# One core's vision transformer block: another order of the steps, and the row maxima transposed in float16

## The chip, the cores and the metric

The kernel runs on one core of one Trainium2 chip. The metric is the device time of one execution, in microseconds; the median of several executions counts.

## The reference, cut to what matters

64 images are computed one by one, and nothing is shared between them but the weights.

```python
h = layernorm(patches(x)) @ W + b          # 768 -> 192, then a second layernorm, class token first: 197 rows
h = h + attention1(layernorm(h))           # 12 heads of 64; q, k scaled by their norm over the heads
h = h + attention2(layernorm(h))           # 12 heads of 16; qkv = x@Wqkv + top-2 gated low-rank term
# attention1: q = q * rsqrt(norm(q, over heads) + eps), k the same
#   softmax(q k^T / scale[h]) v, then @ w_out.T + b_out
# attention2: probs = softmax(x@Wg + bg); two largest gates; h = x@A + ba; delta = 2*((h*gate)@Bm + gate@bb)
#   softmax(q k^T * 16**-0.5) v, then @ Wproj.T + bproj
```

## The kernel before, in words

The 197 rows of an image stand as two tiles of 98 and 99 rows. Five engines work side by side: TensorE (PE) multiplies into the 8 banks of PSUM, VectorE (DVE) and ScalarE (ACT) read the products, GpSimd (POOL) does a few sums and the inverse roots of the layer norms, and SyncE loads and stores images.

All engines walk one list of steps, `ORDER`. The list is one half of a pass, and it is worked off once for each image (64 halves, after some steps ahead and before some behind). Each name is a step: the sign says for which image it is done in this half (none: the half's own image, `+` the next, `-` the one before, `=` two before), the number after the dot is the part, and the number after `@` is the first PSUM bank that the step's product takes. **An engine does its share of the steps strictly in the order of the list.** Semaphores hold it back where an input is not there, or where the bank is not yet read out. The wait for a bank is placed by a helper that looks up the step that used the bank before, and who reads that step's product.

The steps, with what each engine does (the line numbers are those of the profile):

| step | PE | then |
|---|---|---|
| X | | ACT squares the image (L786), POOL sums the squares (L501 to L503) |
| EMB | embedding, float32 (L590, L600) | DVE L1039 to L1046, POOL inverse root (L519, L522) |
| LA, LB, LC | | DVE, two more norms (L1056, L1064, L1069, L1008, L1011, L1017), each with POOL's inverse root between |
| T1, T2 | transposes of the normalised rows (L563) | ACT high half (L796, for T2 L794 too), then DVE low half (L1083) |
| QK.0 to .2 | q and k, two banks each (L612) | ACT squares and copies (L802, L806, L809, L811) |
| S, PS | PS sums over heads (L617) | S: DVE L1094 to L1096; PS: ACT four functions (L822 to L826) |
| N.0 to .3 | | DVE L1102, L1107, L1114; ACT casts (L831) |
| V, V2 | values (L622; L732, L735) | ACT (L835; L890) |
| SM, SM2 | scores for the maxima, 64 rows (L631), 32 rows (L639) | DVE maximum (L1119; twice L1132), the last with the sign change (L1126, L1140) |
| NT, NT2 | transposes of the negated maxima (L552) | ACT (L841, L844) |
| ST, ST2 | scores to exponentiate (L656, L660; L674) | ACT exponentials into four buffers (L850, for ST2 twice) |
| PV, PV2 | sums and values (L686; L744), 32 columns of the array a head | ACT and DVE (L860, L861; L1221, L865, L866), then M and M2: DVE (L1149; L1228) |
| OP, OP2 | output products (L695; L751) | DVE adds (L1158, with variance; L1233) |
| LD, G, GB, T3 | gates (L705), transposes (L552, L713) | DVE L1017, L1167 to L1172, L1177 to L1194, L1200 and L1201 |
| QK2.0, .1 | q and k of the second attention (L722, L725) | ACT L881, L886, L887, then DVE L1207, L1211 |

Three shapes of matmul use the array in parts: SM and ST put two products side by side on 64 rows each, SM2 and ST2 four on 32 rows each, PV and PV2 four on 32 columns each. All others take all rows and columns.

POOL adds the biases in LC and LD (L508, L513), on its own queue and in the order of the list.

Of the kernel before, what the change touches and what calls it, by code (L numbers as in the profile page):

```python
# [27 lines left out]
NT = NP + 1  # L28
PD, KC = 768, 6
TR, TO = 99, 98  # L30
H, DH = 12, 64
# [17 lines left out]


ORDER = """
+X T1@4 =QK2.0@1 =QK2.1@0 QK.0@2 =SM2.0@4 QK.1@0 QK.2@2 =SM2.1@4 -ST.3@0 -ST.4@4 -ST.5@2 -PV.1@6 S
-M.1 =SM2.2@0 -PV.2@4 PS@1 =NT2@7 -M.2 N.0 N.1 N.2 +EMB@2 -OP@3 N.3 =ST2.0@4 V.0@0 SM.0@2 =ST2.1@4
-LD =V2@0 SM.1@4 SM.2@2 -T2@6 =PV2.0@7 SM.3@4 =M2.0 =ST2.2@0 =PV2.1@6 SM.4@4 SM.5@0 -G@7 =PV2.2@2
NT@4 V.1@0 ST.0@4 =M2.1 ST.1@6 +LA =M2.2 -GB +LB ST.2@2 =OP2@5 -T3@4 +LC PV.0@6 M.0
"""


# [17 lines left out]
POS = {p: n for n, p in enumerate(SCHED)}  # L76
# [77 lines left out]
def vit_tower(nc, x_t, w_emb, ln1, ln1_bias, tok_const, tok_bias, w_qk, w_v, w_out, w_gl, w_qkv2, w_lora_b,  # L154
              w_bias2, w_proj, scale, row_const, mats, head_rows, out):
    F32, F16 = mybir.dt.float32, mybir.dt.float16
    ALU, ACT, AX = mybir.AluOpType, mybir.ActivationFunctionType, mybir.AxisListType
    ctx = ExitStack()
    with ctx:
        def sb(name, shape, dt=F32):  # L160
            return ctx.enter_context(nc.sbuf_tensor(name, shape, dt))

        def two(name, shape, dt=F32):
            return [sb(f"{name}{s}", shape, dt) for s in range(2)]
# [25 lines left out]
        ident, pair_sum = mats_sb[:, 0:128], mats_sb[:, 128:256]  # L190
        masks = mats_sb[:, 256:260]
        low_row = sb("low_row", [128, 2])

        bias_rows, low_gates = slice(64, 64 + GROWS), slice(96, 96 + NE + 1)
        one_col = emb_w[:, 0, D:D + 1]
# [37 lines left out]
        vx = [vx_both[0:TR, s] for s in range(2)]  # L233
        ones_col = sb("ones_col", [TR, DH // 2])
        mx = two("mx", [TR, 2, H])
        neg = two("neg", [TR, 2, 128])
        mx2, neg2 = two("mx2", [TR, 2, H]), two("neg2", [TR, 2, 128])
        ebufs = sb("ebufs", [128, EBUFS, 2, 2, NT])
        ebuf = [ebufs[0:TR, i] for i in range(EBUFS)]
        rinv = two("rinv", [128, NT])  # L240
# [101 lines left out]
        def wait(eng, now, sig, p, earlier=None, by=1):  # L342


            n = now.count(steps[sig[0]], p, earlier)
            if n is not None:
                eng.wait_ge(sig[1], n * by)

        def reader(p, bank=None):

            if p[0] in QUAD and bank is not None and bank < BANK[p] + 2:
                return rd_lo[p[0]], p
            return rd_sig[p[0]], ({"PV": "M", "PV2": "M2"}.get(p[0], p[0]), *p[1:])

        def wait_free(eng, now, order, freed):


            q, earlier = now.previous(order, now.at)
            wait(eng, now, *freed(q), earlier)

        def passes(eng, body):
            body(Pass("start", -1))
# [15 lines left out]
        for j in range(4):  # L378
            loads.append((sel2_raw[32 * j:32 * j + 32], head_rows[64:96, 0:G2]))
            for u in range(2):  # L380
                g, r = divmod(head2(u, j), 4)
# [15 lines left out]
        for part in range(3):  # L397
            r = slice(64 + GPITCH * part, 64 + GPITCH * part + NE + 1)
# [17 lines left out]
        def key_rows(t):  # L416
            return TO if t == 0 else TR
# [110 lines left out]
        def _(pe):  # L528
# [4 lines left out]
            for c in range(KC):  # L533
                nc.tensor.matmul(psum[0:TR, spare, D:2 * D], ln1b_raw[:, c, :], emb_raw[:, c, :],
                                 start=(c == 0), stop=(c == KC - 1))
# [12 lines left out]
            def transposes(p, src, width):  # L548

                for t in range(2):  # L550
                    n = key_rows(t)
                    last_mm = nc.tensor.transpose(ps(p, slice(0, width), slice(TO * t, TO * t + n)),  # L552
                                                  src(t, n), ident[0:n, 0:n])
                return last_mm
# [12 lines left out]
            def body(now):  # L567
                for p in now.steps():
# [12 lines left out]
                            pe.wait_ge(setup_dve, 5)  # L581

                    freed = [(b, *now.previous(users[b], p)) for b in banks(p)]
                    for sig, q, earlier in dict.fromkeys((*reader(q, b), earlier) for b, q, earlier in freed):
                        wait(pe, now, sig, q, earlier)
                    if kind == "EMB":
                        pe.wait_ge(x_loaded[s], (now.image(p) + 1) * 16)
                        for t in range(2):
                            for c in range(KC):
                                nc.tensor.matmul(ps(p, slice(0, TR), slice(194 * t, 194 * t + D + 1)),  # L590
                                                 xb[s][:, c, tile_cols(t)], emb_w[:, c, :],
                                                 start=(c == 0), stop=(c == KC - 1))
                        if s == 0 and now.image(p) == 0:
                            for c in range(KC):
                                mm = nc.tensor.matmul(psum[0:TR, spare, 0:D], ones, emb_w[:, c, 0:D],
                                                      start=(c == 0), stop=(c == KC - 1))
                            mm.then_inc(setup_pe, 1)
                        wait(pe, now, xss_ready, ("X", s, 0))
                        for t in range(2):
                            mm = nc.tensor.matmul(ps(p, slice(0, TR), slice(194 * t + 193, 194 * t + 194)),  # L600
                                                  xss[s][:, tile_cols(t)], one_col,
                                                  start=True, stop=True)
                    elif kind == "T1":
                        wait(pe, now, hn_ready, ("LC", s, 0))
                        mm = hidden_transposed(now, p, hn_both[s], hn_doubled, ("LC", s, 0))
                    elif kind == "QK":
                        wait(pe, now, rd_sig["T1"], ("T1", s, 0))
                        for m in range(4):
                            f = 128 * (4 * i + m)
                            at = NT * (m % 2)  # L610
                            for n, (w, v, c) in enumerate(PACKED):
                                mm = nc.tensor.matmul(ps(p, slice(0, 128), slice(at, at + NT), m // 2),  # L612
                                                      qk_w[:, w, f:f + 128], hn_s[s][:, v, c, 0:NT],
                                                      start=(n == 0), stop=(n == 4))
                    elif kind == "PS":
                        wait(pe, now, ss_ready, ("S", s, 0))
                        mm = nc.tensor.matmul(ps(p, slice(0, 128), slice(0, 2 * NT)), pair_sum,  # L617
                                              ss[s][:].rearrange("p a t -> p (a t)"), start=True, stop=True)
                    elif kind == "V":
                        for b in range(2):  # L620
                            for n, (w, v, c) in enumerate(PACKED):
                                mm = nc.tensor.matmul(ps(p, slice(0, TR), slice(0, INNER // 2), b),  # L622
                                                      hn_s[s][:, v, c, tile_cols(i)],
                                                      v_w[:, w, INNER // 2 * b:INNER // 2 * (b + 1)],
                                                      start=(n == 0), stop=(n == 4))
                    elif kind == "SM":
                        wait(pe, now, high_N, ("N", s, 3))
                        for t in range(2):
                            for e in range(2):
                                r = slice(64 * e, 64 * e + 64)  # L630
                                mm = nc.tensor.matmul(ps(p, slice(0, TR), slice(NT * t, NT * t + NT), e),  # L631
                                                      qh[r, i, tile_cols(t)], kh[r, i, 0:NT],
                                                      start=True, stop=True)
                    elif kind == "SM2":
                        wait(pe, now, high_QK2, ("QK2", s, 1))
                        for t in range(2):
                            for j in range(4):
                                r = slice(32 * j, 32 * j + 32)
                                mm = nc.tensor.matmul(ps(p, slice(0, TR), slice(NT * t, NT * t + NT), j),  # L639
                                                      qh2[s][r, i // 2, tile_cols(t)], kh2[s][r, i, 0:NT],  # L640
                                                      start=True, stop=True)
                    elif kind in ("NT", "NT2"):
                        wait(pe, now, mx_ready if kind == "NT" else mx2_ready, p)
                        table = (neg if kind == "NT" else neg2)[s]
                        mm = transposes(p, lambda t, n: table[0:n, t], 128)
                    elif kind == "ST":
                        wait(pe, now, qkn_ready, ("N", s, 3))
                        wait(pe, now, rd_sig["NT"], ("NT", s, 0))
                        for t in range(2):
# [3 lines left out]
                            for n, (left, right) in enumerate(terms):  # L653
                                for e in range(2):
                                    r = slice(64 * e, 64 * e + 64)
                                    nc.tensor.matmul(ps(p, slice(0, TR), slice(NT * t, NT * t + NT), e),  # L656
                                                     left[r], right[r], start=(n == 0), stop=False)
                            for e in range(2):
                                r = slice(64 * e, 64 * e + 64)
                                mm = nc.tensor.matmul(ps(p, slice(0, TR), slice(NT * t, NT * t + NT), e),  # L660
                                                      head_sel[r, 2 * i + e, :], neg_t[s][r, 0:NT],
                                                      start=False, stop=True)
                    elif kind == "ST2":
                        wait(pe, now, rd_sig["QK2"], ("QK2", s, 1))
                        wait(pe, now, rd_sig["NT2"], ("NT2", s, 0))
                        for t in range(2):
# [4 lines left out]
                            for n, (left, right) in enumerate(terms):  # L671
                                for j in range(4):
                                    r = slice(32 * j, 32 * j + 32)
                                    mm = nc.tensor.matmul(ps(p, slice(0, TR), slice(NT * t, NT * t + NT), j),  # L674
                                                          left[r], right[r], start=(n == 0), stop=(n == 3))
                    elif kind == "PV":
                        wait(pe, now, rd_sig["ST"], ("ST", s, 2 * i + 1))
                        wait(pe, now, rd_sig["V"], ("V", s, 1))
                        for c in (2, 0, 1):
                            for t in range(2):  # L680
                                n = key_rows(t)
                                for j in range(4):
# [3 lines left out]
                                    mm = nc.tensor.matmul(  # L686
                                        ps(p, slice(32 * j, 32 * j + 32), slice(NT * (c % 2), NT * (c % 2) + NT), c // 2),
                                        left, eb[0:n, j % 2, t, :], start=(t == 0), stop=(t == 1))
                            if c == 2:
                                mm.then_inc(sums_made[1], 1)  # L690
                    elif kind == "OP":
                        wait(pe, now, rd_sig["PV"], ("M", s, 2))
                        for t in range(2):
                            for m in range(H // 2):
                                mm = nc.tensor.matmul(ps(p, slice(0, TR), slice(D * t, D * t + D)),  # L695
                                                      o_t[s][:, m, tile_cols(t)], out_w[:, m, :],
                                                      start=(m == 0), stop=(m == H // 2 - 1))
                    elif kind == "T2":
                        wait(pe, now, hn2_ready, ("LD", s, 0))
                        mm = hidden_transposed(now, p, hn_both[s], hn2_doubled, ("LD", s, 0))  # L700
                    elif kind == "G":
                        wait(pe, now, rd_sig["T2"], ("T2", s, 0))
                        for t in range(2):
                            for c in range(2):
                                mm = nc.tensor.matmul(ps(p, slice(0, TR), slice(136 * t, 136 * t + 136)),  # L705
                                                      hn2_t[s][:, c, tile_cols(t)], gl_w[:, c, :],
                                                      start=(c == 0), stop=(c == 1))
                    elif kind == "T3":
                        wait(pe, now, hw_ready, ("GB", s, 0))
                        transposes(p, lambda t, n: hw[s][0:n, t], 128)  # L710
                        for t in range(2):
                            n = key_rows(t)
# [24 lines left out]
                    elif kind == "PV2":  # L737
                        wait(pe, now, rd_sig["ST2"], ("ST2", s, i))
                        wait(pe, now, rd_sig["V2"], ("V2", s, 0))
                        for t in range(2):  # L740
                            n = key_rows(t)
# [155 lines left out]
        def _(dve):  # L897
# [58 lines left out]
            def weights_of_scores():  # L956
                split_packed(qk_w, qk_raw)

                nc.vector.tensor_scalar(scale_sb[:], scale_sb[:], WS, None, ALU.mult).then_inc(setup_w, 1)
                splits[0] += 1  # L960
                dve.wait_ge(setup_w, splits[0])
                nc.vector.reciprocal(inv_scale[:], scale_sb[:])
                nc.vector.tensor_copy(head_sel[:], sel_raw.broadcast_to([128, H, TR])
                                      ).then_inc(setup_dve, 1)

# [339 lines left out]
```

## Time and profile before

| | us |
|---|---|
| median of 3 executions | 3112.13 (3110.72 to 3112.16) |
| the profiled execution, its own time | 3109.35 |
| its span, first to last instruction | 3107.6 |
| PE busy in the span | 2962.8 (95%) |
| DVE busy | 2329.0 (75%) |
| ACT busy | 1963.4 (63%) |
| POOL busy | 594.1 (19%) |

Busy means that at least one instruction of the engine is under way. A matmul's record reaches from its start to its modelled end, and the next starts long before that, so what PE needs for a step is read from one step's start to the next one's.

### The profile page before, as it was taken

How to read it: one execution, taken by the hardware profiler on the slowest of the kernel's cores; microseconds unless marked ns; L12 is line 12 of the kernel's file. 1: busy time of each engine (PE TensorE's matmuls, PEld its weight loads, DVE VectorE, ACT ScalarE, POOL GpSimd, SP SyncE). 2: the span in 40 equal slices, each digit the busy share in tenths (PEclk: the TensorE clock that was granted, in tenths of full speed). 3: DMA queues.
4: the chain of work that ended last, by engine and by line, in shares of the span. 5: the costliest groups of instructions: out<-in, count | busy, mean ns of one | idle time of the engine just before them, and what ended most of it. 6: DMA issues, size and time to landing. Idle time of an engine off the chain costs nothing.

```text
span 3107.6 us, 98361 instructions
## 1 busy us (share of the span) xinstructions
PE 2962.8 (95%) x41624; PEld 2428.5 (78%) x41624; DVE 2329.0 (75%) x5441; ACT 1963.4 (63%) x3777; POOL 594.1 (19%) x859
## 2 busy tenths in 40 slices
PE   5899999999999999999999999999999999999996
PEld 4788878877877877877877877888788778778775
DVE  5777777777777777777777777777777777777773
ACT  2566666666666666666666666666666666666663
POOL 3112112111111121121121121121121111111210
PEclk7999999999999999999999999999999999999998
DMA  4000000000000000000000000000000000000000
GB/s 116 9 22 22 12 22 16 17 22 12 21 22 12 21 22 12 22 22 12 22 22 12 22 22 12 22 22 12 22 15 18 22 12 21 22 12 22 14 4 7
DMA packets 28389, 61.28 MB, mean 20 GB/s; under 512 B 4210, under 2 KB 18389, under 8 KB 27958
## 3 DMA queue, kind: packets, MB, share of 16 engines
q1 hardware_dynamic: 27958, 54.98, 6.1%
q8 instruction: 337, 5.52, 0.7%
q14 instruction: 94, 0.77, 0.1%
HBM read 45.29 MB, written 9.68 MB: 18 GB/s over the span
## 4 chain that ended last, share of the span: by engine, by line
PE 59%; DVE 35%; ACT 3%; issue 3%; POOL 0%; DMA 0%; SPq 0%; DVEq 0%; ACTq 0%
PE psum L686 9%; DVE mx L1119 8%; PE psum L695 8%; PE psum L590 8%; PE psum L612 7%; PE psum L674 4%; PE psum L722 4%; PE psum L622 4%; DVE st L1008 3%; PE psum L656 3%; DVE mx L1132 2%; PE psum L725 2%; DVE qk L1211 2%; PE psum L732 2%; PE psum L617 2%
## 5 line engine op out<-in xcount | busy, mean ns | idle before, releaser
L850 ACT ACTIVATE ebufs<-psum 99x788 f32<-99x788 f32 x768 | 592.0, 823 | 57.9 <-PE psum L674 45.2
L519 POOL TENSOR_TENSOR veps<-mv,eps_ln 99x2 f32<-99x2 f32 x256 | 116.7, 456 | 2266.5 <-DVE mv L1041 1344.9
L1132 DVE TENSOR_REDUCE mx<-psum 99x4 f32<-99x788 f32 x384 | 357.5, 974 | 137.5 <-PE psum L639 137.2
L1119 DVE TENSOR_REDUCE mx<-psum 99x4 f32<-99x788 f32 x384 | 362.9, 974 | 52.1 <-PE psum L631 52.1
L612 PE MATMUL psum<-hn_s,qk_w 128*128 128x197 f16 x3840 | 354.1, 249 | 14.9 <-DVE hn_s L1083 7.4
L612 PEld LDWEIGHTS psum<-hn_s,qk_w 128*128 128x128 f16 x3840 | 322.2, 97 | 35.6 <-DVE qk L1211 19.0
L686 PE MATMUL psum<-ebufs,vx 98*32 98x197 f32 (+1 forms) x6144 | 293.7, 330 | 0.0
L590 PE MATMUL psum<-emb_w,xb 128*99 128x193 f32 x1536 | 264.0, 327 | 0.0
L695 PE MATMUL psum<-out_w,qk 128*99 128x192 f32 x1536 | 263.8, 328 | 0.1
L590 PEld LDWEIGHTS psum<-emb_w,xb 128*99 128x99 f32 x1536 | 249.1, 166 | 1.4 <-issue 0.9
L686 PEld LDWEIGHTS psum<-ebufs,vx 98*32 98x32 f32 (+1 forms) x6144 | 201.4, 110 | 57.2
L695 PEld LDWEIGHTS psum<-out_w,qk 128*99 128x99 f32 x1536 | 245.1, 166 | 0.3 <-issue 0.3
L622 PE MATMUL psum<-v_w,hn_s 128*99 128x384 f16 x1280 | 233.9, 330 | 0.0
L656 PE MATMUL psum<-qh,kh 64*99 64x197 f16 x1536 | 207.9, 255 | 17.9 <-DVE mx L1132 17.0
L1102 DVE TENSOR_TENSOR qk<-qk,ss 128x1182 f32<-128x1182 f32 x64 | 89.1, 1392 | 167.3 <-ACT ss L826 167.3
L802 ACT ACTIVATE qk_sq<-psum 128x788 f32<-128x788 f32 x192 | 158.8, 827 | 70.3 <-PE psum L612 70.3
L656 PE MATMUL psum<-ql,kh 64*99 64x197 f16 x1536 | 201.6, 245 | 0.0
L660 PE MATMUL psum<-neg_t,head_sel 64*99 64x197 f16 x1536 | 201.4, 245 | 0.0
L656 PE MATMUL psum<-qh,kl 64*99 64x197 f16 x1536 | 201.3, 245 | 0.0
L622 PEld LDWEIGHTS psum<-v_w,hn_s 128*99 128x99 f16 x1280 | 154.8, 127 | 47.2
L831 ACT CAST kh<-qk 128x1182 f16<-128x1182 f32 x64 | 75.5, 1180 | 176.4 <-DVE qk L1107 176.4
L1149 DVE TENSOR_TENSOR qk<-psum,rinv 128x394 f32<-128x394 f32 x192 | 108.9, 567 | 101.8 <-ACT rinv L861 62.1
(172 smaller groups left out, 6442.7 us busy)
## 6 DMA issues: line engine op xcount, KB each, us to landing
xb<-x_t SPq DMA_DIRECT2D x64, 591.0 KB, 3.8
out<-h SPq DMA_DIRECT2D x128, 73.5 KB
out<-h SPq DMA_DIRECT2D x64, 0.8 KB
vx<-w_qk SPq DMA_DIRECT2D x2, 384.0 KB, 7.8
qk_sq<-w_emb SPq DMA_DIRECT2D x1, 576.0 KB
vx<-w_qk SPq DMA_DIRECT2D x1, 576.0 KB, 5.6
out_w<-w_out SPq DMA_DIRECT2D x8, 72.0 KB
late<-w_lora_b SPq DMA_DIRECT2D x1, 480.0 KB
```

Source lines behind the costliest of these rows:

```text
L590: nc.tensor.matmul(ps(p, slice(0, TR), slice(194 * t, 194 * t + D + 1)), xb[s][:, c, tile_cols(t)], emb_w[:, c, :], start=(c == 0), stop=( ...
L612: mm = nc.tensor.matmul(ps(p, slice(0, 128), slice(at, at + NT), m // 2), qk_w[:, w, f:f + 128], hn_s[s][:, v, c, 0:NT], start=(n == 0), s ...
L622: mm = nc.tensor.matmul(ps(p, slice(0, TR), slice(0, INNER // 2), b), hn_s[s][:, v, c, tile_cols(i)], v_w[:, w, INNER // 2 * b:INNER // 2 ...
L656: nc.tensor.matmul(ps(p, slice(0, TR), slice(NT * t, NT * t + NT), e), left[r], right[r], start=(n == 0), stop=False)
L660: mm = nc.tensor.matmul(ps(p, slice(0, TR), slice(NT * t, NT * t + NT), e), head_sel[r, 2 * i + e, :], neg_t[s][r, 0:NT], start=False, sto ...
L674: mm = nc.tensor.matmul(ps(p, slice(0, TR), slice(NT * t, NT * t + NT), j), left[r], right[r], start=(n == 0), stop=(n == 3))
L686: mm = nc.tensor.matmul(ps(p, slice(32 * j, 32 * j + 32), slice(NT * (c % 2), NT * (c % 2) + NT), c // 2), left, eb[0:n, j % 2, t, :], sta ...
L695: mm = nc.tensor.matmul(ps(p, slice(0, TR), slice(D * t, D * t + D)), o_t[s][:, m, tile_cols(t)], out_w[:, m, :], start=(m == 0), stop=(m ...
L802: nc.scalar.activation(qk_sq[:, 4 * i:4 * i + 4, :].rearrange("p (b m) t -> p b (m t)", b=2), src, ACT.Square, scale=1 / WS)
L850: nc.scalar.activation(ebuf[n].rearrange("p e a t -> p e (a t)"), psum[0:TR, b + 2 * half:b + 2 * half + 2, 0:2 * NT], ACT.Exp).then_inc(r ...
L1119: nc.vector.tensor_reduce(mx[s][:, :, 2 * i:2 * i + 2].rearrange("p a e -> p e a"), psum[0:TR, b:b + 2, 0:2 * NT].rearrange("p e (a t) -> ...
L1132: nc.vector.tensor_reduce(mx2[s][:, :, at:at + 2].rearrange("p a e -> p e a"), psum[0:TR, b + 2 * half:b + 2 * half + 2, 0:2 * NT].rearran ...
```

## The change

The list of steps is another one: other neighbours, other banks, and T1, NT, SM.4, SM.5, ST.0 to ST.2, PV.0, M.0 and T3 are done in another half relative to their image. The tables of the negated maxima (`neg`, `neg2`) become float16, and their transposes NT and NT2 are float16 matmuls with a float16 identity, which DVE makes once. A helper `release` is put around the two look-ups of who frees a bank or buffer; it corrects the count of a semaphore where the freeing step stands later in the list than the waiting one.

```diff
 ORDER = """
-+X T1@4 =QK2.0@1 =QK2.1@0 QK.0@2 =SM2.0@4 QK.1@0 QK.2@2 =SM2.1@4 -ST.3@0 -ST.4@4 -ST.5@2 -PV.1@6 S
--M.1 =SM2.2@0 -PV.2@4 PS@1 =NT2@7 -M.2 N.0 N.1 N.2 +EMB@2 -OP@3 N.3 =ST2.0@4 V.0@0 SM.0@2 =ST2.1@4
--LD =V2@0 SM.1@4 SM.2@2 -T2@6 =PV2.0@7 SM.3@4 =M2.0 =ST2.2@0 =PV2.1@6 SM.4@4 SM.5@0 -G@7 =PV2.2@2
-NT@4 V.1@0 ST.0@4 =M2.1 ST.1@6 +LA =M2.2 -GB +LB ST.2@2 =OP2@5 -T3@4 +LC PV.0@6 M.0
+=T3@5 -SM.4@0 -SM.5@6 QK.0@2 QK.1@4 QK.2@6 =QK2.0@2 -NT@1 S =QK2.1@4 -ST.0@6 -ST.1@2 -ST.2@0 -ST.3@6
+-PV.0@2 +X -M.0 =SM2.0@4 -ST.4@0 PS@3 -ST.5@4 =SM2.1@0 -PV.1@6 -PV.2@2 -M.1 N.0 -M.2 =SM2.2@4 N.1
+N.2 +EMB@1 N.3 =NT2@2 -OP@6 =ST2.0@0 =ST2.1@4 +LA -LD =V2@1 SM.0@4 SM.1@2 +LB V.0@6 -T2@4 =ST2.2@0
+=PV2.0@6 =PV2.1@7 +LC -G@5 =M2.0 =PV2.2@4 SM.2@0 V.1@2 =M2.1 =M2.2 -GB SM.3@0 +T1@7 =OP2@4
 """
...
+        ident_h = sb("ident_h", [TR, TR], F16)
...
-        neg = two("neg", [TR, 2, 128])
-        mx2, neg2 = two("mx2", [TR, 2, H]), two("neg2", [TR, 2, 128])
+        neg = two("neg", [TR, 2, 128], F16)
+        mx2, neg2 = two("mx2", [TR, 2, H]), two("neg2", [TR, 2, 128], F16)
...
+        def release(q, freed, earlier):
+
+            sig, r = freed
+            assert earlier or POS[r] >= POS[q]
+            return sig, r, earlier and POS[r] >= POS[q]
+
         def wait_free(eng, now, order, freed):
             q, earlier = now.previous(order, now.at)
-            wait(eng, now, *freed(q), earlier)
+            wait(eng, now, *release(q, freed(q), earlier))
...
-                    for sig, q, earlier in dict.fromkeys((*reader(q, b), earlier) for b, q, earlier in freed):
+                    for sig, q, earlier in dict.fromkeys(release(q, reader(q, b), earlier) for b, q, earlier in freed):
                         wait(pe, now, sig, q, earlier)
...
                         table = (neg if kind == "NT" else neg2)[s]
-                        mm = transposes(p, lambda t, n: table[0:n, t], 128)
+                        for t in range(2):
+                            n = key_rows(t)
+                            mm = nc.tensor.matmul(ps(p, slice(0, 128), slice(TO * t, TO * t + n)),
+                                                  table[0:n, t], ident_h[0:n, 0:n], start=True, stop=True)
...
                 nc.vector.reciprocal(inv_scale[:], scale_sb[:])
+                nc.vector.tensor_copy(ident_h[:], ident[0:TR, 0:TR])
```

## Rows read from the trace of the kernel before

**Rows 1.** The page: busy us, share of the span and instructions of each engine.

```profile
PE 2962.8 (95%) x41624; PEld 2428.5 (78%) x41624; DVE 2329.0 (75%) x5441; ACT 1963.4 (63%) x3777; POOL 594.1 (19%) x859
```

**Rows 2.** Timeline of PE, same step one image apart (start; us from first start to last end).

```profile
1500.18 4.10 PE L590 MATMUL psum<-emb_w,xb 128*99 128x193 f32 x24
...
1547.19 4.10 PE L590 MATMUL psum<-emb_w,xb 128*99 128x193 f32 x24
```

**Rows 3.** Timeline of PE, shapes that meet: scores, values, transposes.

```profile
1511.04 0.37 PE L631 MATMUL psum<-kh,qh 64*99 64x197 f16 x4
1511.34 0.46 PE L674 MATMUL psum<-qk 32*99 32x197 f16 x12
...
1513.61 0.55 PE L631 MATMUL psum<-kh,qh 64*99 64x197 f16 x8
1514.09 0.56 PE L563 MATMUL psum<-mats_sb,hn 98*128 98x98 f32 x4
...
1541.63 0.88 PE L686 MATMUL psum<-ebufs,ones_col 98*32 98x197 f32 x16
1542.33 1.53 PE L686 MATMUL psum<-ebufs,vx 98*32 98x197 f32 x32
1543.79 0.38 PE L639 MATMUL psum<-qk 32*99 32x197 f16 x8
...
1547.01 0.34 PE L552 MATMUL psum<-mats_sb,neg 98*128 98x98 f32 x2
```

**Rows 4.** Timeline of PE, where a step stood waiting.

```profile
1515.39 0.37 PE L631 MATMUL psum<-kh,qh 64*99 64x197 f16 x4
1516.11 0.46 PE L674 MATMUL psum<-qk 32*99 32x197 f16 x12 [0.34 <-issue]
...
1538.98 0.29 PE L656 MATMUL psum<-qh,kh 64*99 64x197 f16 x2
...
1540.14 0.29 PE L656 MATMUL psum<-qh,kh 64*99 64x197 f16 x2 [0.28 <-DVE mx L1132]
```

**Rows 5.** Timeline of DVE, after the output product and in the second part of a half.

```profile
1555.97 0.55 DVE L1158 TENSOR_TENSOR h<-psum,h 99x384 f32<-99x384 f32 x1
...
1557.38 1.36 DVE L1114 TENSOR_TENSOR kl<-qk,kh 128x1182 f16<-128x1182 f32 x1
...
1561.04 1.86 DVE L1119 TENSOR_REDUCE mx<-psum 99x4 f32<-99x788 f32 x2 [0.78 <-PE psum L631]
1562.82 0.56 DVE L1083 TENSOR_TENSOR hn_s<-psum,hn_s 128x394 f16<-128x394 f32 x1
...
1568.49 0.73 DVE L1056 SCALAR_TENSOR_TENSOR lnt<-lnt,rstd,emb_b 99x192 f32<-99x192 f32 x2
...
1570.08 0.33 DVE L1228 TENSOR_TENSOR late<-psum,late 128x197 f32<-128x197 f32 x1
...
1572.22 0.74 DVE L1064 SCALAR_TENSOR_TENSOR h<-lnt,mv,tokc 99x192 f32<-99x192 f32 x2
...
1574.59 0.53 DVE L1233 TENSOR_TENSOR h<-psum,h 99x384 f32<-99x384 f32 x1
```

**Rows 6.** Timeline of POOL: inverse roots and a bias.

```profile
1557.54 1.25 POOL L519 TENSOR_TENSOR veps<-mv,eps_ln 99x2 f32<-99x2 f32 x1 [1.08 <-DVE mv L1011]
...
1560.34 1.00 POOL L513 TENSOR_TENSOR h<-h,rowc 99x384 f32<-99x384 f32 x1 [0.79 <-DVE hn L1017]
...
1574.76 0.19 POOL L519 TENSOR_TENSOR veps<-mv,eps_ln 99x2 f32<-99x2 f32 x1 [3.54 <-DVE mv L1011]
1575.03 0.69 POOL L522 TENSOR_TENSOR rstd<-veps,half_neg 99x2 f32<-99x2 f32 x1
```

**Rows 7.** Timeline of ACT: the four functions of PS, the next step, exponentials.

```profile
1547.21 0.59 ACT L822 ACTIVATE ss<-psum,tiny 128x394 f32<-128x394 f32 x1 [1.44 <-PE psum L617]
...
1549.49 0.31 ACT L844 CAST neg_t<-psum 128x197 f16<-128x197 f32 x1
...
1556.41 1.55 ACT L850 ACTIVATE ebufs<-psum 99x788 f32<-99x788 f32 x2 [0.24 <-PE psum L674]
```

## The prediction, made before the changed kernel was run

> **What bounds the kernel now.** I read the page first, then the timelines of each engine over two neighbouring images, then the table of waits for the places where PE stands. PE is busy 95% of the span, DVE 75%, ACT 63% [rows 1]. The timeline of PE repeats: EMB starts at 1500.18 and at 1547.19, so one image takes 47.01 us [rows 2]. 64 of these are 3008.6 us, and 99.0 of the span's 3107.6 us are the setup, the first steps and the last ones. So nearly all of the time is 64 times one half of a pass, and the question is how long a half gets.
>
> A half of 47.0 us is PE's work plus PE's standing. The standing is seen by comparing a step's length (from its first start to the next step's) with the same step where nothing held it. SM.3 takes 0.72 us from 1515.39 to 1516.11, while a lone SM takes 0.30 (1511.04 to 1511.34): 0.4 us lost, since ST2.2's four banks include the one that DVE still reads SM.3 from [rows 3, 4]. ST.3 takes 1.16 us (1538.98 to 1540.14), and unhindered ones 0.69: 0.47 lost, again a bank of which DVE has yet to take the maximum [rows 4]. Five more places follow the same pattern (SM.4, PV.0, SM2.0, the QK steps, T1). By the timeline I count 1.8 us for all seven. PE's own work is then about 45.2 us. Had PE never to wait, the kernel would take 1.8 x 64 = 115 us less.
>
> **The change part by part.** *Neighbours of one shape.* A lone SM takes 0.30 us, but the pair SM.1, SM.2 takes 0.48 (1513.61 to 1514.09) and not 0.60: the step in front of one of its own shape is about 0.09 shorter [rows 3]. PV shows it too: sums and values, of one shape, stand 0.70 apart for 16 matmuls; 32 should then take twice 0.66 + 0.03 = 1.35, and take 1.46 (1542.33 to 1543.79) ahead of SM2 [rows 3]. So a change of shape costs 0.09 to 0.11 us. The old list changes shape 27 times in a half, the new one 24 times (new pairs: SM.0/SM.1, ST.0 to ST.3 in a row, PV.1/PV.2, ST2.0/ST2.1, PV2.0/PV2.1; lost ones: those of the old ST.3 to ST.5 and SM.1/SM.2). 3 x 0.10 = 0.3 us less. ST2.0/ST2.1 and PV2.0/PV2.1 don't stand together in this trace; from nothing to 0.13 each are the bounds, and I take 0.1. The Trainium skill says the same (TensorEngine Tiling (Array Packing), Key Properties: a change of tiling mode drains the engine) without a price.
>
> *NT and NT2 in float16.* In float32 the step takes 0.18 us (1547.01 to 1547.19) for two matmuls [rows 3]. No float16 matmul of this size stands in the trace. The bounds are no change (0.18) and half of it (0.09, as float16 takes half the time for a column in all steps here: 0.085 us for QK's 197 columns against 0.165 for OP's 192); I take 0.11, which is 0.14 us less in a half for two steps. They are also ready sooner for ACT, which is worth nothing by itself. The added identity is one DVE copy in the setup, under 1 us, once.
>
> *PE's work in the new list.* 45.2 - 0.3 - 0.14 = 44.8; summing the new list step by step from the unhindered lengths gives 44.6. I take 44.7.
>
> *Where PE will stand.* I laid the new list out from QK.0 = 0 with the lengths above and asked of each step when its banks and inputs are free. QK takes 1.71 a step, so QK2.0 starts at 5.1, NT at 6.5, ST.0 at 8.1, PV.0 at 10.9, PS at 14.2, EMB at 20.8. ACT keeps up behind QK: NT's copy ends near 7.9, ST.0's exponential at 9.9 (0.78 each [rows 7]), so ST.0 and ST.3, which wait for these, have 0.15 us to spare. Then:
> - ACT runs PS before ST.5. PS takes 2.28 us from 1547.21 to 1549.49 [rows 7]; in the new list that is 15.15 to 17.43, and ST.5's exponential ends at 18.25. PV.2 would start at 18.15: 0.16 us of standing, and behind PV.2 in PE's queue stand SM2.2 and EMB, which shift with it; DVE's N steps, which wait for PS alone, don't. SM2.1 waits for PS's bank: 0.10.
> - ST2.1 and V2 follow ST2.0 at once, while ACT needs two exponentials of 0.78 for each ST2. V2 takes a bank of ST2.0's lower half: 0.31. SM.0 and V.0 take banks of ST2.1: 0.10 and 0.27.
>
> Together 0.94 us, against 1.8 before: ST2.2 no longer stands behind a maximum that it must outwait, and ST.3 and ST.4 no longer take banks straight behind a maximum. By this path a half is 44.7 + 0.94 = 45.6 us.
>
> *DVE's own path.* The new list piles work on DVE between OP and the next half. OP's product is ready at 29.2 by my layout. From there, in order: OP with variance 1.41 (1555.97 to 1557.38), LA 1.59 (1568.49 to 1570.08), LD 0.58, SM.0 and SM.1 1.78 (1561.04 to 1562.82), LB 2.37 (1572.22 to 1574.59), and M2.2 with GB 2.14 (1570.08 to 1572.22) [rows 5]; the rest by the same view's starts: T2 0.48, three shuffles 0.8, LC 0.58, G 0.77, two M2 0.54, SM.2 and SM.3 1.78, T1 0.57. Sum 15.4, with 0.4 us for waits on PE (SM.0, G): T1 ends at 45.1. SM.5 takes T1's bank, and it must start 0.30 before QK.0. So this path gives 45.1 + 0.3 = 45.4, with no reserve against the other.
>
> *GpSimd beside DVE.* The addition in front of the inverse root takes 0.19 us at 1574.76 but 1.25 at 1557.54, where DVE's L1114 runs from 1557.38 for 1.36 [rows 5, 6]: POOL got nothing done until DVE's instruction was over. In the old list that stood on a path with room. In the new list POOL's additions for OP fall under LA: two instructions, 0.73 us together [rows 5]. Addition until 0.8 and then 0.69 for the power [rows 6]: 1.5 after the variance. LD follows LA's 1.59: hidden by a hair. POOL's bias of LC takes 1.00 us [rows 6] and lies over DVE's subtraction in G, which reads two tiles of SBUF. If POOL has come first and DVE waits, that is up to 0.3 on DVE's path. No row of this trace shows DVE waiting so; the bounds are nothing and 0.3, and I take the upper one, since the path has no reserve.
> The Trainium skill (SBUF — State Buffer, Who interferes with whom) says that a DVE instruction with two inputs in SBUF and a GpSimd instruction that reads SBUF shut each other out, the first to issue winning. The row at 1557.54 agrees with the half of it that stops GpSimd. By the page, DVE would lose the 0.3 in G too, and a half would be 45.7; without it, 45.6.
>
> The sums of X move from beside T1 to after PV.0, over maxima of SM2; their rows are far from any wait in both lists, and ACT's square (1.17) has room. SP loads the next image at QK.0 as before, a whole half and more ahead of the X that reads it, and its stores still follow OP2; neither meets POOL's queue. The setup and the drain I leave at 99.0; the steps ahead gain T1 and the tail loses little; 3 us either way.
>
> **Sum.** One half 45.7. Span 64 x 45.7 + 99.0 = 3023.8; the profiled execution's own time is 1.75 above its span and the median 2.8 above that: 3028.4, taken as 3029.
>
> **Rivals.**
> - *The waits are hidden better than I count.* ACT's exponentials or DVE's maxima have room that I gave away (0.94 counted of which 0.68 behind ST2). A half of 45.0 gives 64 x 45.0 + 103.5 = 2984. For it: three of the waits are of 0.1 us. Against: DVE's path alone is 45.4.
> - *DVE's path becomes the bound.* Its instructions overlap by 0.1 us back to back; where semaphores part them, whole durations count, and my chain has 24 parts. 16.6 for 15.4 gives a half of 46.4 and 3073. The signs would be PE standing at SM.5 or QK.0 for T1. For it: from LA on DVE has no pause longer than 0.2 us by my layout.
> - *Slower: GpSimd and DVE shut each other out on that same path.* If the two POOL operations for OP are held over the whole of LA (1.59) and not only over its first pair, LD comes 0.7 to 0.8 later; the same for LB's root before LC under T2 and the shuffles (0.5), and 0.3 in G. The path is then 45.4 + 1.6 = 47.0 or more, and it decides against the change from 1.6 us a half on: at 47.15, 3121. For it: the 1.25 us row. Against it: the addition at 1574.76 ran undisturbed beside an instruction with one input in SBUF and one in PSUM, which most of these are.
> - *Nothing gained.* Shorter switches and the same standing elsewhere: the half stays within 0.1 of 47.0. It needs 2.3 us of standing where I count 0.94.
>
> **How the numbers follow.** Forecast (45.4 to 46.0 a half, 3010 to 3048) 0.48; better hidden 0.12; DVE the bound (46.0 to 46.9, 3048 to 3105) 0.27; no change 0.04; slower 0.09. About 0.2% (6 us, 0.1 us a half) is what a measurement can tell from no change. Faster 0.87, same 0.04, slower 0.09. The range for 8 in 10 runs from 2995 to 3098: it leaves out most of the second case and the slower one.
>
> **What would show it.** In the timeline of the changed kernel: EMB to EMB 45.7; ST2.0 to ST2.1 about 0.70 and PV2.0 to PV2.1 about 0.70; V2 and V.0 waiting for L850; PV.2 waiting for L850 behind L826; DVE without pause from SM.0 to T1; NT at 0.11. The prediction is wrong if PE waits over 0.5 us at SM.5 or QK.0, if POOL's L519 after OP stands longer than 0.8, or if new waits stand in the QK and ST stretch, where I have only 0.15 us of room at four places.

## The result

The changed kernel takes 3044.46 us (3043.56 to 3049.03) against 3112.13 us, a ratio of 0.979 (95% interval 0.9775 to 0.9799): faster by 68 us, where 83 were forecast. The first profiled execution of the changed kernel ran with matmuls about twice as long (5833 us, with a recorded granted clock of 1.00), so the profile below is of a further execution of the same kernel, which took 3045.52 us.

The page of the changed kernel, its parts 1, 2 and 4 (the whole of the span; busy us and share, busy tenths, the chain that ended last):

```profile
span 3042.7 us, 98360 instructions
PE 2922.2 (96%) x41624; PEld 2428.9 (80%) x41624; DVE 2331.0 (77%) x5442; ACT 1927.0 (63%) x3777; POOL 537.5 (18%) x859
...
PE   5899999999999999999999999999999999999996
...
PE 70%; DVE 22%; ACT 3%; issue 3%; POOL 1%; DVEq 0%; ACTq 0%
```

By busy shares little has happened: PE 96% for 95% [rows 1], DVE 77% for 75%. The chain that ended last says more: 22% of it lies on DVE (PE 70%). In the kernel before it was 35% (PE 59%), a number of its page that the prediction didn't use. The gain is seen only from one image to the next. The timeline of PE after, two EMB one image apart and what lies between them at the places that the prediction names:

```profile
1615.47 4.18 PE L595 MATMUL psum<-emb_w,xb 128*99 128x193 f32 x24
1619.49 0.43 PE L605 MATMUL psum<-emb_w,xss 128*99 128x1 f32 x4
1619.78 0.25 PE L652 MATMUL psum<-ident_h,neg 98*128 98x98 f16 x2
1619.87 4.11 PE L703 MATMUL psum<-out_w,qk 128*99 128x192 f32 x24
...
1630.80 1.55 PE L752 MATMUL psum<-ebufs,v 98*32 98x197 f32 x32
1632.47 1.14 PE L713 MATMUL psum<-gl_w,ss 128*99 128x136 f32 x8
...
1637.16 2.11 PE L759 MATMUL psum<-proj_w,late 128*99 128x192 f32 x12
1639.11 0.34 PE L557 MATMUL psum<-mats_sb,gl 98*128 98x98 f32 x2
...
1639.77 0.90 PE L636 MATMUL psum<-kh,qh 64*99 64x197 f16 x8
1640.60 5.29 PE L617 MATMUL psum<-hn_s,qk_w 128*128 128x197 f16 x60
...
1661.40 0.90 PE L595 MATMUL psum<-emb_w,xb 128*99 128x193 f32 x4
```

From 1615.47 to 1661.40 are 45.93 us, where it was 47.01 [rows 2] and 45.7 was forecast. The three QK steps stand together and fill 1.71 us each without a wait (all three are the line at 1640.60). The float16 transpose takes 0.09 us (1619.78 to 1619.87), half of before [rows 3]. What stands out is the end of a half: T3 begins at 1639.11 and takes 0.44 us of PE where nothing waits behind it (in `more_op2`, below), but SM.4 starts only at 1639.77: 0.22 us of standing. SM.4 with SM.5 takes 0.83 us to QK.0, where a pair takes 0.48 [rows 3]: 0.35 us more. What PE waits for there is seen on DVE. Its timeline from OP to T1 (start, us, line, what ended its idle time):

```profile
1624.11 0.56 DVE L1167 TENSOR_TENSOR h<-psum,h 99x384 f32<-99x384 f32 x1 [0.95 <-PE psum L703]
...
1625.52 0.71 DVE L1065 SCALAR_TENSOR_TENSOR lnt<-lnt,rstd,emb_b 99x192 f32<-99x192 f32 x2
...
1627.09 0.64 DVE L1026 TENSOR_SCALAR hn<-h,mv,rstd 99x192 f32<-99x192 f32 x2
1627.64 1.86 DVE L1128 TENSOR_REDUCE mx<-psum 99x4 f32<-99x788 f32 x2
1629.42 0.73 DVE L1073 SCALAR_TENSOR_TENSOR h<-lnt,mv,tokc 99x192 f32<-99x192 f32 x2
...
1633.65 0.44 DVE L1176 TENSOR_TENSOR gl<-psum,rowc 99x272 f32<-99x272 f32 x1
1634.13 0.17 DVE L1180 TENSOR_REDUCE gmax<-gl 99x2 f32<-99x16 f32 x1
1634.33 0.41 DVE L1181 TENSOR_TENSOR gl<-gl,gmax 99x16 f32<-99x16 f32 x1
...
1638.74 0.97 DVE L1128 TENSOR_REDUCE mx<-psum 99x4 f32<-99x788 f32 x1
1639.63 0.56 DVE L1092 TENSOR_TENSOR hn_s<-psum,hn_s 128x394 f16<-128x394 f32 x1
...
1670.04 0.56 DVE L1167 TENSOR_TENSOR h<-psum,h 99x384 f32<-99x384 f32 x1 [0.95 <-PE psum L703]
```

After its wait of 0.95 us for OP, DVE waits for no engine by this view until T1 is read at 1640.19. SM.3's maximum ends at 1639.71 and PE starts SM.4, on that bank, at 1639.77; T1 is read at 1640.19, and SM.5, on that bank, can start then (its first matmul starts at 1640.29). The last line is OP's addition one half later. So a half is a ring: PE from QK.0 to OP's product, DVE from OP's addition to T1, and back to PE by the bank of SM.5 and by T1's product, which QK.0 reads.

### The profile page after: what moved, and what is told of

It reads as the page before. It is cut to its first block, busy times and chain, and to the rows that moved or that the text cites. A ratio compares the mean times of both kernels' runs of the same rounds, so it can differ in the third digit from the quotient of the medians.

```text
span 5831.5 us, 98360 instructions
## 1 busy us (share of the span) xinstructions
PE 5773.1 (99%) x41624; PEld 3665.4 (63%) x41624; DVE 2364.8 (41%) x5442; ACT 2000.0 (34%) x3777; POOL 627.9 (11%) x859
## 4 chain that ended last, share of the span: by engine, by line
PE 98%; DVE 1%; ACT 0%; issue 0%; POOL 0%; DVEq 0%
PE psum L694 15%; PE psum L617 12%; PE psum L595 9%; PE psum L703 9%; PE psum L627 8%; PE psum L664 7%; PE psum L752 5%; PE psum L682 5%; PE psum L759 5%; PE psum L730 4%; PE psum L668 2%; PE psum L636 2%; PE psum L733 2%; PE psum L713 2%; PE psum L740 2%; PE psum L622 2%
## 5 line engine op out<-in xcount | busy, mean ns | idle before, releaser
L617 PE MATMUL psum<-hn_s,qk_w 128*128 128x197 f16 x3840 | 711.5, 397 | 7.8 <-DVE hn_s L1092 4.1
L617 PEld LDWEIGHTS psum<-hn_s,qk_w 128*128 128x128 f16 x3840 | 539.6, 149 | 173.7 <-issue 16.1
L694 PE MATMUL psum<-ebufs,vx 98*32 98x197 f32 (+1 forms) x6144 | 606.8, 582 | 0.0
L595 PE MATMUL psum<-emb_w,xb 128*99 128x193 f32 x1536 | 562.2, 565 | 0.0
L703 PE MATMUL psum<-out_w,qk 128*99 128x192 f32 x1536 | 555.2, 564 | 0.0
L627 PE MATMUL psum<-v_w,hn_s 128*99 128x384 f16 x1280 | 475.4, 556 | 0.9 <-DVE mx L1128 0.9
L694 PEld LDWEIGHTS psum<-ebufs,vx 98*32 98x32 f32 (+1 forms) x6144 | 317.6, 163 | 239.5 <-issue 36.7
L694 PE MATMUL psum<-ebufs,ones_col 98*32 98x197 f32 (+1 forms) x3072 | 316.8, 564 | 0.0
L668 PE MATMUL psum<-neg_t,head_sel 64*99 64x197 f16 x1536 | 306.0, 389 | 0.0
L664 PE MATMUL psum<-ql,kh 64*99 64x197 f16 x1536 | 302.5, 388 | 0.0
```

The costliest lines, as they stand in the source:

```text
L694: mm = nc.tensor.matmul(ps(p, slice(32 * j, 32 * j + 32), slice(NT * (c % 2), NT * (c % 2) + NT), c // 2), left, eb[0:n, j % 2, t, :], sta ...
```

## The experiments

All times are medians beside runs of the kernel before on the same chip (3111.5 to 3112.3). "A half" is the time from EMB to the next EMB on PE's timeline, from here on the median over the whole profiled execution: 47.01 us for the kernel before, 45.94 for the changed one.

### The two parts of the change

`after_again` is the changed kernel as it is; its profile is the one above (3045.52 us in its one run).

> The changed kernel once more, for an undisturbed profile. By my forecast EMB to EMB is about 45.7 us, ST2.0 to ST2.1 and PV2.0 to PV2.1 about 0.70 us, PE waits behind the exponentials at V2 and V.0, and DVE has no pause from SM.0 to T1. By the measured 3044 us the half is nearer to 46.0: if DVE's path is what is longer, PE waits at SM.5 or QK.0 for T1; if it is PE's work, the unhindered steps are longer than I summed.

Half right: the half is 45.94, PE waits for T1 at SM.5, and DVE is the longer path. The unhindered lengths were right within 0.1 us. PV2.0 to PV2.1 is 0.69 us, but ST2.0 to ST2.1 is 0.87 and not 0.70: ST2.1 takes OP's banks, which DVE reads until 1624.67, and starts at 1624.77.

`f16_only` is the kernel before, with this edit of the change alone (and the copy of the identity):

```diff
-        neg = two("neg", [TR, 2, 128])
+        neg = two("neg", [TR, 2, 128], F16)
...
-                        mm = transposes(p, lambda t, n: table[0:n, t], 128)
+                        for t in range(2):
+                            n = key_rows(t)
+                            mm = nc.tensor.matmul(ps(p, slice(0, 128), slice(TO * t, TO * t + n)),
+                                                  table[0:n, t], ident_h[0:n, 0:n], start=True, stop=True)
```

> The kernel before with nothing changed but the maxima's tables and transposes in float16. If a float16 transpose takes PE 0.11 instead of 0.18 us and no wait absorbs it: 0.14 us a half, 9 us less (ratio 0.997). Rival: in the old order NT stands behind DVE's maxima and in front of V.1, which waits too, so that only NT2's half counts, 4 us less (0.9985); or the weight load sets the length and nothing is gained (1.000).

3108.04 us, ratio 0.9989 (0.9980 to 0.9998): 4 us faster, as the first rival said. PE's timeline of this kernel, NT with V.1 behind it, then NT2 with EMB behind it:

```profile
1520.52 0.26 PE L648 MATMUL psum<-ident_h,neg 98*128 98x98 f16 x2
1520.62 1.79 PE L623 MATMUL psum<-v_w,hn_s 128*99 128x384 f16 x10
...
1547.08 0.25 PE L648 MATMUL psum<-ident_h,neg 98*128 98x98 f16 x2
1547.17 1.03 PE L591 MATMUL psum<-emb_w,xb 128*99 128x193 f32 x5
```

NT itself falls from 0.23 to 0.10 us and NT2 from 0.18 to 0.09. In the old order PE waits behind V.1 anyway, for ACT's copy of NT, which ACT does only after work that came before it in its queue. This wait grows by as much as NT loses: V.1 to ST.0 is 1.91 us for 1.79 in the kernel before. Only NT2's part is left, and the half falls by 0.04 us.

`order_only` is the changed kernel without these edits, so the new list alone.

> The changed kernel with the maxima transposed in float32 as before: only the new order. By my sum it is 9 us slower than the changed kernel, about 3053 (ratio 0.981). Rival: a longer NT holds ST.0 (which has 0.15 us of room behind ACT's copy of NT) and this runs through the whole half, so that the order alone is worth less: 3060 or more (0.984).

3058.67 us, ratio 0.9831 (0.9817 to 0.9844): the order is worth 53 us, and float16 another 14 in the new order against 4 in the old one. The expectation was 3053 and the rival's 3060 or more; 3058.67 lies between the two. Both transposes now lie on PE's part of the ring. NT2 in this kernel, from PE's timeline:

```profile
1625.02 0.37 PE L556 MATMUL psum<-mats_sb,neg 98*128 98x98 f32 x2
1625.23 4.06 PE L699 MATMUL psum<-out_w,qk 128*99 128x192 f32 x24
1629.22 0.46 PE L678 MATMUL psum<-qk 32*99 32x197 f16 x12
```

It takes 0.21 us against 0.09, while OP takes 3.99 (1625.23 to 1629.22) against 4.03 behind the float16 NT2: 0.08 net, and NT (0.17 against 0.09) as much again. That is 0.16 us a half, which is what the half grows by (46.10), and 10 of the 14 us; the spans of the two profiled executions differ by 10.6. The rival, a delay at ST.0 that runs through the whole half, isn't needed. How the 53 us of the order divide into fewer changes of shape and less standing was not tried by itself.

### Is it a ring, or PE's work as a whole?

Two kernels put the same short matmul between two PV steps of one shape. `split_pv` does it between PV.1 and PV.2, `split_pv2` between PV2.0 and PV2.1. The first one's edit:

```diff
+                        if i == 2:
+                            nc.tensor.matmul(ps(p, slice(0, TR), slice(0, 1), 1), ident[:, 0:TR], one_col,
+                                             start=True, stop=True)
                         for c in (2, 0, 1):
```

> The changed kernel with one more matmul (all rows and columns, one moving column, its product overwritten) between PV.1 and PV.2, so that these two of one shape are parted. My theory after the profile: the half is a ring, PE from SM.5 over QK, ST, PV and EMB to OP, then DVE from OP's addition to T1, whose bank and product SM.5 and QK.0 need. PV.1 and PV.2 lie on PE's part of it, so the join that is lost (0.11 us) and the matmul itself with its second switch (0.1 to 0.3) count in full: 0.2 to 0.4 us a half, 13 to 26 us slower than the changed kernel, 3058 to 3071. Rival (PE's whole queue is the bound): the same.

> The same matmul between PV2.0 and PV2.1 instead. My theory: this stretch lies beside DVE's part of the ring, and PE stands there anyway (0.17 us or more at G, 0.5 at T3 and SM.4), so nothing is lost: 3043 to 3048. Rival, that PE's work as a whole is the bound: 13 to 26 us slower, as for the pair PV.

`split_pv`: 3071.88 us, 27 more than the changed kernel (ratio to before 0.9871, 0.9855 to 0.9887). Its PE timeline at the place:

```profile
1624.81 1.52 PE L697 MATMUL psum<-ebufs,vx 98*32 98x197 f32 x32
1626.27 0.33 PE L688 MATMUL psum<-emb_w,mats_sb 128*99 128x1 f32 x2
1626.53 0.88 PE L697 MATMUL psum<-ebufs,ones_col 98*32 98x197 f32 x16
```

PV.1's values now take 1.46 us (1.34 in the changed kernel, where PV.2 follows at once) and the matmul 0.26: 0.38 us for two changes of shape and one column. All of it arrives in the half (46.33). The change of shape at the price of about 0.11 us that the prediction took from PV [rows 3] is confirmed for joined PV steps. Ring and rival forecast the same here, so this run shows that the stretch counts in full, and doesn't decide between them.

`split_pv2`: 3056.31 us, 12 more (0.9819, 0.9805 to 0.9834). My expectation of nothing failed, and the time is only 1 us below what the rival gave; the trace tells more than the time. PE's timeline there, then DVE's second shuffle of M2:

```profile
1636.29 0.88 PE L755 MATMUL psum<-ebufs,v 98*32 98x197 f32 x16
1637.10 0.33 PE L749 MATMUL psum<-emb_w,mats_sb 128*99 128x1 f32 x2
1637.36 0.88 PE L755 MATMUL psum<-ebufs,v 98*32 98x197 f32 x16
1638.16 1.17 PE L713 MATMUL psum<-gl_w,ss 128*99 128x136 f32 x8
```
```profile
1638.31 0.01 DVE L1233 LOAD_MASK_SELECT late<-psum  x1 [0.19 <-PE psum L755]
```

From PV2.0 to G it takes 1.87 us, 0.20 more than after the change (1630.80 to 1632.47), since a wait of 0.17 us for T2 at G took up part of 0.37. DVE, which went through this stretch without a wait, now stands 0.19 us at the shuffle for PV2.1's product, and G begins 0.12 us behind LC's end and not 0.02. From T2 to G DVE takes 2.09 us (1637.28 to 1639.37) for 1.86. Behind it the subtraction beside GpSimd's bias becomes 0.09 shorter (0.32 for 0.41 us), so 0.14 reach the half (46.08), where PE's work as the bound would have given 0.37. The stretch beside DVE's part of the ring has room, but only up to the next product that DVE needs.

`more_op2` tests a stretch whose product DVE takes late: two more matmuls of 192 columns ahead of OP2.

```diff
+                        for t in range(2):
+                            nc.tensor.matmul(ps(p, slice(0, TR), slice(D * t, D * t + D)),
+                                             ident[:, 0:TR], proj_w[:, t, :], start=True, stop=True)
```

> The changed kernel with two more matmuls of 192 columns in float32 (0.165 us each, overwritten) ahead of OP2: 0.33 us more work for PE in each half, in the stretch between T1 and SM.4, where PE stands 0.53 us. My theory (the ring passes by this stretch, DVE's OP2 and T3 come later than PE's): nothing, 3043 to 3047. Rival (PE's work as a whole is the bound): 21 us slower, 3065.

3053.46 us (0.9809, 0.9793 to 0.9826), 9 more, where I had expected nothing and the rival 21. PE's timeline:

```profile
1639.85 0.81 PE L758 MATMUL psum<-proj_w,mats_sb 128*99 128x192 f32 x4
1640.50 2.11 PE L762 MATMUL psum<-proj_w,late 128*99 128x192 f32 x12
1642.45 0.34 PE L557 MATMUL psum<-mats_sb,gl 98*128 98x98 f32 x2
...
1642.89 0.55 PE L636 MATMUL psum<-kh,qh 64*99 64x197 f16 x8
```

The two recorded as four and took 0.65 us, twice what I had put down. SM.4 now follows T3 after 0.44 us and SM.4 with SM.5 takes 0.48: the whole wait is gone. So 0.57 of the 0.65 us cost nothing, and the half grows by 0.08 (46.02), which is 5 of the 9 us; the other 4 lie outside the steady halves (from the last PS to the end the profile has 106.8 us for 101.2). This speaks for the ring; PE's work as the bound would have cost 42 us.

### Shorten the ring

`pool_late` moves GpSimd's addition of LC behind the gates:

```diff
-                    elif p[0] == "LC":
+                    elif p[0] == "T1":

-                        wait(pool, now, hn_ready, p)
+                        wait(pool, now, hn_ready, ("LC", s, 0))
+                        wait(pool, now, hw_ready, ("GB", s, 0))
```

> The changed kernel with GpSimd's bias addition of LC (1.00 us) done at T1 behind the gates instead of at LC, so that it no longer lies over DVE's subtraction L1181, which takes 0.41 us there and 0.175 in the kernel before. My theory: DVE lost 0.24 us to GpSimd's read, on the ring: 0.24 us a half, 15 us faster than the changed kernel, about 3030. Rivals: the subtraction stays at 0.41 (its length is not due to GpSimd), or DVE has the room and the time stays at 3044.

3031.91 us (0.9740, 0.9725 to 0.9754), 13 less than the changed kernel; the half is 45.70, 0.24 shorter. POOL's timeline in the changed kernel, the inverse root's addition under LA and the bias of LC:

```profile
1625.68 0.27 POOL L524 TENSOR_TENSOR veps<-mv,eps_ln 99x2 f32<-99x2 f32 x1 [3.66 <-DVE mv L1020]
1633.70 1.00 POOL L513 TENSOR_TENSOR h<-h,rowc 99x384 f32<-99x384 f32 x1 [0.78 <-DVE hn L1026]
```

The timelines of `pool_late`, DVE's subtraction and then POOL's bias:

```profile
1534.24 0.18 DVE L1182 TENSOR_TENSOR gl<-gl,gmax 99x16 f32<-99x16 f32 x1
```
```profile
1538.64 0.99 POOL L514 TENSOR_TENSOR h<-h,rowc 99x384 f32<-99x384 f32 x1 [5.81 <-DVE gl L1204]
```

In the changed kernel the subtraction started at 1634.33 and ended at 1634.74, just after GpSimd (1634.70). With GpSimd's addition out of the way it takes 0.18 us. So here GpSimd came first and DVE waited, 0.23 us, which the trace of before could not show. The Trainium skill (SBUF — State Buffer, Who interferes with whom) has both directions, and the traces agree with both: GpSimd held at 1557.54 [rows 6], DVE held here.

`ring_short` takes SM.5 off T1's bank:

```diff
-=T3@5 -SM.4@0 -SM.5@6 QK.0@2 QK.1@4 QK.2@6 =QK2.0@2 -NT@1
+=T3@5 -SM.4@0 -SM.5@2 QK.0@6 QK.1@4 QK.2@2 =QK2.0@0 -NT@1
```

> The changed kernel with other banks: SM.5 on 2 and 3 in place of T1's 7, QK.0 on 6, QK.2 on 2, QK2.0 on 0. SM.5 no longer waits until DVE has read T1; QK.0 still does. My theory: PE does SM.5 (0.30 us) while DVE ends T1, the ring is 0.29 us shorter, 18 us less: about 3026. Rival, that PE's own queue is the bound and the standing at SM.4 and SM.5 only shifts: 3044. If a new bank wait arises at ST.0 or ST.2, it shows as PE's wait there and takes back part.

3032.70 us (0.9745, 0.9730 to 0.9759), 12 less; the half is 45.67, 0.27 shorter. PE's timeline:

```profile
1585.35 0.34 PE L721 MATMUL psum<-mats_sb,comb 98*41 98x98 f32 x2
1585.83 0.55 PE L636 MATMUL psum<-kh,qh 64*99 64x197 f16 x8
1586.39 1.78 PE L617 MATMUL psum<-hn_s,qk_w 128*128 128x197 f16 x19
```

SM.4 and SM.5 now take 0.56 us to QK.0 instead of 0.83. Right in the half; 18 us were expected in all, and about 6 are lost outside the steady halves.

`ring_pool` has both edits.

> Both of the edits that helped: SM.5 on other banks and GpSimd's bias addition at T1. The ring falls by 0.275 + 0.24 us to about 45.42 us a half, and PE's queue without its standing at T3 and SM.4 is 45.41: the two meet, the gain is nearly the sum of both, 33 us less than the changed kernel, about 3011. Rival: one edit uses up the room, and the second brings under 0.1 us a half: 3026 or more.

3017.83 us (0.9696, 0.9682 to 0.9711). Its half is 45.42, as expected, 0.52 below the changed kernel; of the 33 us that this is worth, 27 are in the total. The chain that ended last now lies on PE with 88% and on DVE with 2%. The rest is in the drain. Stretches from the last PS to the end, first of the changed kernel, then of `ring_pool` (busy us of each engine, PE's granted clock, DMA):

```profile
2941.48:3000.00 58.52, 51.05 (x791) 40.57 (x790) 35.82 (x74) 28.51 (x55) 2.79 (x5) 0.94 0.02 5
3000.00:3042.70 42.70, 23.55 (x344) 18.76 (x342) 16.83 (x50) 15.44 (x35) 1.00 (x1) 0.87 0.03 8
```
```profile
2909.13:2967.65 58.52, 50.77 (x746) 40.33 (x744) 34.84 (x69) 26.49 (x52) 1.90 (x3) 0.91 0.02 5
2967.65:3017.10 49.45, 30.57 (x394) 24.32 (x386) 17.81 (x55) 17.51 (x37) 1.90 (x3) 0.75 0.03 7
```

The same steps take 101.2 us in the one and 108.0 in the other, with the granted clock at 0.94 and 0.87 against 0.91 and 0.75, between its two levels of 1.2 and 2.4 GHz, after PE had begun to idle between steps. At least a part may belong to the execution and not to the kernel: the four executions of `ring_pool` range from 3013.17 us (mean granted clock 0.989) to the profiled one's 3019.30 (0.986).

`st5_first` adds one exchange to `ring_pool`:

```diff
--ST.4@0 PS@3 -ST.5@4
+-ST.4@0 -ST.5@2 PS@4
```

> The kernel ring_pool with ST.5 ahead of PS (ST.5 on banks 2 and 3, PS on 4): ST.4 and ST.5 are neighbours of one shape, and ACT no longer runs PS's four functions before ST.5's exponential. Two changes of shape less (0.18 us) and 0.18 us of standing at ST.5 gone, but SM2.1 now waits for ST.5's exponential, by my count 0.2 us. Net 0 to 0.15 us a half: 3002 to 3011. Rival: SM2.1's wait is longer, since it also holds the maximum that DVE takes ahead of N.0: 3011 to 3030.

3012.74 us (0.9683, 0.9668 to 0.9697), the lowest median; its half is 45.36. PE's timeline from PS on:

```profile
1635.88 0.93 PE L623 MATMUL psum<-ss,mats_sb 128*128 128x394 f32 x2
1636.95 0.38 PE L645 MATMUL psum<-qk 32*99 32x197 f16 x8
1637.26 0.88 PE L695 MATMUL psum<-ebufs,ones_col 98*32 98x197 f32 x16
```

ST.4 takes 0.72 us for 0.81 in `ring_pool`, and ST.5 0.78 for 0.95, but PS 1.07 (from 1635.88) for 0.86, since SM2.1 now waits about 0.2 us. Counted in the two lists it is one change of shape less, and not the two of the expectation. 0.05 us a half are 3 us; the difference of 5 in the medians is within the two intervals.

## Why the prediction was right, and where it was off

- **What a half is made of.** Right: 64 halves hold the time, and the half fell from 47.01 to 45.94.
- **The waits on PE.** V2 and V.0 do wait for exponentials, 0.13 and 0.21 us where 0.31 and 0.27 were forecast, and SM2.1 about 0.15 for PS (0.10). SM.0 and PV.2 don't wait, and ST2.1 does, 0.17 us for DVE's reading of OP. With 0.17 at G and the 0.22 and 0.35 before QK.0 PE stands 1.4 us in a half, where 0.94 was forecast; by the same count its own work is 44.5 (forecast 44.7). The waits behind OP and the joins ST2.0/ST2.1, SM.0/SM.1 and PV2.0/PV2.1 lie beside DVE's part of the ring. They set nothing in the changed kernel as long as DVE's next product is in time (`more_op2`, `split_pv2`).
- **The two paths.** The text weighed PE's own path (45.6) and DVE's (45.7 with GpSimd) as equals. Without the standing at SM.4 and SM.5 PE's path is 45.37 (45.94 - 0.22 - 0.35), so DVE's was the longer one. "DVE's path becomes the bound" was a rival: its sign, PE standing at SM.5 for T1, came (though not the 0.5 us there that would have made the prediction wrong by its own words), at 45.94 a little below its range of 46.0 to 46.9. Its reason, that DVE's chain of instructions is longer than summed, did not come true: the chain fits the sum.
- **The terms that were mis-sized.** Three stretches make the ring. DVE's OP to the end of T1: 16.08 us (1624.11 to 1640.19), forecast 15.9 (its terms sum to 15.8) and 0.3 for GpSimd, so 0.1 less. T1 to QK.0: 0.41, forecast 0.30. QK.0 to OP's addition: 29.44 (1640.60 to 1670.04), forecast 29.2. EMB stands where it was put, at 20.80 (1640.60 to 1661.40), but takes 4.31 us (1615.47 to 1619.78) and not the 4.23 of before, and DVE starts 4.24 us after OP's first matmul, where the forecast's numbers leave 4.06 (29.2 less 20.8, 4.23 and 0.11). The two stretches at PE were 0.35 us too short in all, and DVE's 0.1 too long.
- **The sum.** 3028.4 forecast; 64 x 0.24 = 15.4 for the half; setup and drain 102.5 instead of 99.0 (the first half takes 47.9 us where the old one took 43.8, by the starts of PS); the median is 1.8 above the span and not 4.5. 3028.4 + 15.4 + 3.5 - 2.8 = 3044.5. That the forecast came this close is in part luck: the 0.3 us for GpSimd had no row behind it, and the last two terms nearly cancel.
- **GpSimd and DVE.** The upper bound of 0.3 us in G was right to take: 0.24. The slower rival didn't come. GpSimd's addition for OP ran from 1625.68 to 1625.95, under LA's pair (0.71 us from 1625.52): 0.27 us, 0.08 more than alone, and not 0.73 or more. It did not have to wait for the end of the pair.
- **Float16.** 0.09 us, the lower bound and not the 0.11 taken. It pays on the ring (14 us in the new order), and hardly in the old one (4 us), which the sum of step lengths could not tell apart.
- **X's sums** lie beside maxima read from PSUM in the new order (and beside reads from PSUM in the old one). No wait hangs on them in either trace; that part of the order was not tried by itself, and neither was the helper that corrects the counts.

## What to carry to other kernels

When several engines work off fixed queues, look for the ring that one period closes: here PE, then DVE, then PE by a bank. A tenth of a microsecond counts in full on it, and half a microsecond beside it costs nothing until it reaches the next product that the ring needs. After laying out a new order, sum each path of the ring and not only the busiest engine, and look how much of the chain that ended last lies on the others (35% on DVE already before); and look at the last hand-over of a period first, since exchanging four bank numbers there brought 12 us.

## What was not expected of the hardware

- The length of a float32 step depends on what stands in front of it: EMB takes 4.23 us behind the float32 NT2 (1500.18 to 1504.41 in the kernel before), 4.26 in `f16_only` (1500.21 to 1504.47) behind the float16 NT2, and 4.31 in the changed kernel behind SM2.2, which is float16 and of another shape. OP takes 3.99 behind the float32 NT2, 4.03 behind the float16 one. So part of what a float16 transpose saves is paid by its neighbour. But OP takes 4.05 behind EMB in the kernel before (1504.41 to 1508.46), and both are float32, so the type alone is not the cause. Why is open.
- GpSimd's addition took 0.27 us beside two DVE instructions that stood back to back, while one long DVE instruction, also with two inputs in SBUF, held it for 1.25 us [rows 6].
- The same final steps took 101 and 108 us in two kernels at different granted clocks. The difference is half of what one of the two ring edits is worth in the total.
